# A quantized gated FFN on one core: the gate row fetched by DMA, weight chunks held for x 0, tile 1's results on ScalarE and GpSimd, and the up codes of tile 3 ahead of tile 2's results

## The reference

```
h   = gelu(cond @ W0 + b0);  h = gelu(h @ W1 + b1);  att = softmax(h @ W2 + b2)
y   = einsum(att, weight)[b] @ x[b] + att @ bias_k                      # 128 x 2048, per tile
qg, sg = quant(bf16(y) * inv_gate);   qu, su = quant(bf16(y) * inv_up)  # row max / 127, round, clip
gate = (qg @ w_gate.T) * sg * s_wgate;   up = (qu @ w_up.T) * su * s_wup      # 2048 -> 1024
inter = bf16(clip(silu(gate) * up, -10, 10));   qi, si = quant(inter * inv_inter)
out  = x + (qi @ w_down.T) * si * s_wdown                                     # 1024 -> 2048
```

## Time and profile before

| | |
|---|---|
| median of the timed runs | 824.15 us |
| the profiled execution, as a whole | 823.83 us |
| its span, first to last instruction | 822.0 us |
| TensorE matmul busy | 789.6 us (96%) |
| VectorE busy | 722.2 us (88%) |
| ScalarE busy | 437.4 us (53%) |
| GpSimd busy | 150.7 us (18%) |
| granted TensorE clock, mean | 0.997 of full speed |
| DMA | 117.72 MB, mean 143 GB/s |

### The profile page before, as it was taken

One profiled execution on the slowest core, in us unless ns is written; L12 is line 12 of the kernel. 1 busy time (PEld: TensorE's weight loads), 2 busy tenths in 40 slices (PEclk: granted clock), 3 DMA queues, 4 the chain that ended last, 5 costly groups with the idle time before them and its releaser, 6 DMA issues.

```text
span 822.0 us, 9083 instructions
## 1 busy us (share of the span) xinstructions
PE 789.6 (96%) x3437; PEld 360.1 (44%) x3504; DVE 722.2 (88%) x825; ACT 437.4 (53%) x370; POOL 150.7 (18%) x142
## 2 busy tenths in 40 slices
PE   5689999899999999999999999999999999999997
PEld 2344444344444444444444444444444444444443
DVE  5888898998988888898888899888889888888967
ACT  2556426655556654555665455566555556645441
POOL 3560200222210222221022222012222101222000
PEclk9999999999999999999999999999999999999999
DMA  9995252654544555444435554444545444454332
GB/s 251 232 217 103 52 205 52 166 167 141 160 147 116 109 160 167 141 145 141 138 102 166 161 143 145 122 138 124 167 146 161 141 116 123 147 167 141 100 106 103
DMA packets 158196, 117.72 MB, mean 143 GB/s; under 512 B 147524, under 2 KB 147652, under 8 KB 148807
## 3 DMA queue, kind: packets, MB, share of 16 engines
q1 hardware_dynamic: 156424, 104.55, 42.4%
q0 software_dynamic: 1728, 12.58, 7.7%
HBM read 59.44 MB, written 33.55 MB: 113 GB/s over the span
## 4 chain that ended last, share of the span: by engine, by line
PE 82%; DVE 11%; DMA 3%; ACT 2%; issue 1%; SPq 0%; POOL 0%; DVEq 0%
PE down_ps L584 24%; PE gate_ps L512 23%; PE up_ps L512 23%; PE conv_ps L456 11%; DVE amax L901 3%; DMA wd<-rows 2%; DMA qgT<-qg 1%; ACT qg L690 1%; DVE region L919 1%; DVE region L1012 1%; DVE region L996 1%; DVE region L930 1%; DVE region L1002 1%; DVE region L955 1%; DVE aggw L896 0%
## 5 line engine op out<-in xcount | busy, mean ns | idle before, releaser
L512 PE MATMUL gate_ps<-wg,qgT 128*128 128x512 bf16 x987 | 219.1, 379 | 1.6 <-ACT qgT L714 1.4
L512 PE MATMUL up_ps<-wu,quT 128*128 128x512 bf16 x931 | 215.0, 379 | 3.2 <-ACT quT L722 1.6
L584 PE MATMUL down_ps<-wd,qiT 128*128 128x512 bf16 x884 | 209.1, 379 | 3.6 <-ACT qiT L772 2.1
L901 DVE TENSOR_REDUCE amax<-region 128x1 f32<-128x2048 f32 (+1 forms) x93 | 178.8, 1923 | 1.3
L364 POOL TENSOR_TENSOR prod<-wexp,att_bc 128x1024 f32<-128x1024 f32 x29 | 55.5, 1913 | 558.5 <-DVE region L941 540.5
L512 PEld LDWEIGHTS gate_ps<-wg,qgT 128*128 128x128 bf16 x992 | 96.7, 98 | 119.1 <-issue 3.2
L584 PEld LDWEIGHTS down_ps<-wd,qiT 128*128 128x128 bf16 x912 | 88.9, 98 | 128.2 <-issue 29.7
L512 PEld LDWEIGHTS up_ps<-wu,quT 128*128 128x128 bf16 x960 | 93.7, 98 | 114.8 <-ACT quT L722 1.8
L456 PE MATMUL conv_ps<-xt,aggw 128*128 128x512 f32 x256 | 122.4, 602 | 8.2 <-DMA xt<-x 6.2
L690 ACT ACTIVATE qg<-region,recip 128x2048 f16<-128x2048 f32 x30 | 60.1, 2002 | 129.9 <-DVE recip L911 129.9
L679 ACT ACTIVATE y<-conv_ps,aggb 128x512 bf16<-128x512 f32 x120 | 81.8, 686 | 79.6 <-PE conv_ps L456 75.0
(11 more groups left out here) (117 smaller groups left out, 488.8 us busy)
## 6 DMA issues: line engine op xcount, KB each, us to landing
xt<-x SPq DMA_DIRECT2D x31, 1024.0 KB, 4.8
out<-xt SPq DMA_DIRECT2D x30, 1024.0 KB, 4.0
wg<-w_gateT POOLq DMA_DIRECT2D x4, 1024.0 KB, 13.4
wu<-w_upT POOLq DMA_DIRECT2D x4, 1024.0 KB, 19.0
wd<-w_downT POOLq DMA_DIRECT2D x4, 1024.0 KB, 7.3
out<-xt SPq DMA_DIRECT2D x2, 512.0 KB, 2.7
xt<-x SPq DMA_DIRECT2D x2, 512.0 KB, 3.7
out<-xt SPq DMA_DIRECT2D x4, 256.0 KB, 2.7
```

The source lines that it names most:

```text
L512: last = nc.tensor.matmul(acc[:, n * BANK:(n + 1) * BANK], codes[:, k * P:(k + 1) * P], wts[:, k, n * BANK:(n + 1) * BANK], start=(k == 0) ...
L584: last = nc.tensor.matmul(down_bank(t, c), qiT_at(t)[:, k * P:(k + 1) * P], wd[:, k, c * BANK:(c + 1) * BANK], start=(k == 0), stop=(k == ...
L901: nc.vector.tensor_reduce(amax[:, i:i + 1], src, axis=AX.X, op=ALU.max, apply_absolute_value=True).then_inc(max_ready, 1)
```

## The change

It has four parts.

1. The gate row is no longer in `rows` but an input of its own, and a DMA on SyncE's queue writes it to all 128 partitions, right behind x 0. x 1 comes next, then the remaining rows.
2. GpSimd waits for x 0 before it issues the gate weight chunks, and issues all four at once. The spreads of the other six rows follow.
3. On VectorE tile 1's gate scaling (`quant_g(1)`) comes before the first softmax piece of the later tiles, and on ScalarE the exponential of these comes after tile 1's codes.
4. The results of tile 1 leave VectorE: ScalarE takes each piece out of PSUM times the row scale (`scaled_out`), GpSimd multiplies by the column scale and adds x. These eight GpSimd operations stand ahead of its mixture for tile 5. TensorE turns the up codes of tile 3 right behind down 1, not behind down 2; ScalarE rounds and empties them accordingly, ahead of `conv_out(4)`. Up values of tile 3 get the second half of `region1`, so that only the clip waits for ScalarE to have read `region2`; tile 5's gate scaling then waits for the inner codes of tile 3.

```diff
-        INVG, INVU, SWG, SWU, INVI, SWD = 2, 3, 4, 5, 6, 8
+        INVU, SWG, SWU, INVI, SWD = 1, 2, 3, 4, 6
+        scaled1 = [prod[:, 4 * i:4 * i + 4, :].rearrange("p k o -> p (k o)") for i in range(2)]
 # up_at
+            if t == EARLY:
+                return region1[:, I:H]
 # SyncE, start
             sp.dma_start(xslot(0), x[0, :, :]).then_inc(x_in[0], 16)
-            sp.dma_start(rows_s, rows[:, 0:6 * I]).then_inc(rows_in[0], 16)
-            sp.dma_start(invi_s, rows[:, 6 * I:7 * I]).then_inc(rows_in[1], 16)
+            sp.dma_start(invg_bc[:, :], inv_gate.partition_broadcast(P)).then_inc(invg_in, 16)
+            sp.dma_start(xslot(1), x[1, :, :]).then_inc(x_in[1], 16)
+            sp.dma_start(rows_s, rows[:, 0:4 * I]).then_inc(rows_in[0], 16)
+            sp.dma_start(invi_s, rows[:, 4 * I:5 * I]).then_inc(rows_in[1], 16)
...
-            sp.dma_start(xslot(1), x[1, :, :]).then_inc(x_in[1], 16)
 # SyncE, store(t)
-                sp.wait_ge(result_ready, NC * (t + 1))
+                if t == 1:
+                    sp.wait_ge(second_result, NC)
+                else:
+                    sp.wait_ge(result_ready, NC * t)
 # GpSimd
-            load(wg, w_gateT, 0, wg_in)
-            load(wg, w_gateT, 1, wg_in)
+            pool.wait_ge(x_in[0], 16)
+            for i in range(WCH):
+                load(wg, w_gateT, i, wg_in)
             pool.wait_ge(rows_in[0], 16)
-            spread(invg_bc[:, 0:I], rows_s[:, 0:I])
-            spread(invg_bc[:, I:H], rows_s[:, I:H])
-            load(wg, w_gateT, 2, wg_in)
-            load(wg, w_gateT, 3, wg_in)
...
+            pool.wait_ge(row_spread, SWD)
+            for c in range(NC):
+                cols = slice(c * BANK, (c + 1) * BANK)
+                pool.wait_ge(scaled_ready, NC + c + 1)
+                nc.gpsimd.tensor_tensor(scaled1[c % 2], scaled1[c % 2], swd_bc[:, cols], ALU.mult).then_inc(product_step, 1)
+                pool.wait_ge(product_step, c + 1)
+                nc.gpsimd.tensor_tensor(xcols(1, c), xcols(1, c), scaled1[c % 2], ALU.add).then_inc(second_result, 1)
             for t in range(5, B):
                 if t == 5:
-                    pool.wait_ge(prod_ready, 2)
+                    pool.wait_ge(second_result, NC)
 # TensorE, conv: which PSUM release a piece waits for
                     elif t == 4 and c < 2:
-                        pe.wait_ge(uturn_out, UTURN["i", 1 + c] + 1)
-                    elif t == 5 and c < 2:
                         pe.wait_ge(uturn_out, UTURN["u", 3] + 1 + c)
 # TensorE, order
                 down(1, c)
+            turn_u(3)
             down(2, 0)
             down(2, 1)
             conv(4)
             down(2, 2)
             down(2, 3)
-            turn_u(3)
             up(3)
 # ScalarE
+            def scaled_out(c):
+                if c == 0:
+                    act.wait_ge(iscale_ready, 2)
+                    act.wait_ge(prod_ready, 2)
+                    act.wait_ge(scaled_ready, NC)
+                if c >= 2:
+                    act.wait_ge(second_result, c - 1)
+                act.wait_ge(down_done, NC + c + 1)
+                nc.scalar.activation(scaled1[c % 2], down_bank(1, c), ACT.Copy, scale=tscale(1, 2)).then_inc(scaled_ready, 1)
...
+            quant_g(1)
             act.wait_ge(att_dve, 12)
             nc.scalar.activation(group(eatt, 1), group(logits, 1), ACT.Exp).then_inc(exp_done, 1)
-            quant_g(1)
...
             turned_i(2)
+            scaled_out(0)
+            scaled_out(1)
+            quant_u(3)
+            scaled_out(2)
+            scaled_out(3)
+            turned_u(3)
             conv_out(4)
-            quant_u(3)
-            turned_u(3)
 # VectorE, quant(t), up_out(t), clip(t), down_out(t, c)
+                if t == EARLY + 2:
+                    dve.wait_ge(icodes_ready, EARLY + 1)
...
-                else:
+                elif t > EARLY:
                     dve.wait_ge(ucodes_ready, t + 2)
...
+                if t == EARLY:
+                    dve.wait_ge(ucodes_ready, t + 2)
...
+                if t == 2 and c == 0:
+                    dve.wait_ge(scaled_ready, 2 * NC)
 # VectorE, order
+            quant_g(1)
             softmax_in(1, B - FIRST, 9)
-            quant_g(1)
...
-            for t in range(2):
-                for c in range(NC):
-                    result(t, c)
+            for c in range(NC):
+                result(0, c)
             quant_u(3)
```

More of the change, by code:

```diff
@@ L3, with adaln_ffn @@
 from contextlib import ExitStack
-def adaln_ffn(nc, x, mlp, b2, weightT, w_gateT, w_upT, w_downT, rows, out):
+def adaln_ffn(nc, x, mlp, b2, weightT, w_gateT, w_upT, w_downT, inv_gate, rows, out):
     fp32 = mybir.dt.float32
@@ L184, in adaln_ffn @@
         row_spread = sem("row_spread")
+        invg_in = sem("invg_in")
         ones_set = sem("ones_set")
```

25 lines of the change are left out of this document (12 added, 13 removed).

## The result

The changed kernel took 820.03 us (median of six runs, 818.36 to 821.73), beside 824.08 us for the kernel before on the same chip: a ratio of 0.9947, 95% interval 0.9931 to 0.9962. The forecast was 821.2. The profiled execution took 818.36 us, 5.47 less than the one of before, while the medians are 4.05 apart. The six times are 818.36, 818.38, 820.01, 820.05, 820.16 and 821.73: they lie in steps of about 1.7 us, and the profile shows the lowest.

A forecast was written before the change was run, and what follows sets the result against it. Once the pipeline runs TensorE's matmuls bind, so only its earlier idle and slow time counts: 2.05 us (start) plus 0.9 (middle) is 2.95, giving 820.9 for the profiled execution, median 821.2, range 816.5 to 823.2.

The forecast's parts named there:

- Weight chunks and x 0: Start: with chunks held, x 0 lands at about 8 and conv 0 starts at 10.75, 3.15 us earlier, at full clock.
- Tile 0's codes: VectorE in the start: factor at 19.9, codes, turns and gate 0 6.6 us earlier, a gain that does not last.
- Tile 1's codes: Deciding term: spreads start at about 21.2, product at 29.2, TensorE turns tile 1's codes at 36.2, 3.05 us earlier.
- the walk over boundaries: VectorE's four remaining mixing steps pass one at each boundary between GpSimd's spreads, at 24, 25.6, 27.2 and 28.3.
- The rival with about 6 us for the code: GpSimd's code load by the page: spreads start at 17, tile 1's codes turned at 34.8, 1.4 us more gain.
- The clock: TensorE idle 4.3 us before turning tile 1's codes, then half clock: of the 3.05 us gain 2.05 is kept.
- Rival 1: No slow clock after TensorE's idle time in the start: gain 3.95 us, 820.2 us; chance 0.17.
- Between 45 and 89 us: Order unchanged, so the start's shift is carried; up loads some 3 us later, hidden unless they slip over 5 us.
- The middle: 89 to 150 us: tile 1's results off VectorE, tile 3's up values moved; gain 0.9 us, between -1 and 1.7.
- 2: Spreads start after 23, behind mixing and product: tile 1's codes turned at 31.9, 816 us; chance 0.20 with intermediates.
- 4: GpSimd's eight operations meet VectorE at 3.20 us each, conv 5 10 us late, about 831; 0.08 with milder delays.
- 3: VectorE's mixing delays GpSimd's descriptors, so all chunks and x 2 slip 5 us: 820.8 to 822.3; chance 0.10.

The follow-up runs named there:

- the repeat: The changed kernel run once more, unaltered: median 819.70 us, ratio 0.9940 to the kernel before; its profiled execution took 820.15 us.
- code early: Changed kernel plus one tiny partition_broadcast, read by nothing, on GpSimd ahead of its wait for x 0: 818.67 us.
- mixing held: Changed kernel, but GpSimd's mixing of conv 5's weights also waits for VectorE's product of tile 4: 819.56 us.
- x 2 early: Changed kernel, but the load of x 2 is issued right behind the rows instead of behind gate chunk 0: 820.18 us.
- fillers ahead of turn 0: Unread matmuls in TensorE's idle time before turning tile 0's codes; alone on the changed kernel, with three more before conv 2: 818.99 us; three combined kernels: 817.53 to 818.99.

## Why the prediction was right, and where its terms were off

- **Weight chunks and x 0.** Conv 0 at 10.81 for 10.75, full clock (but see the slow start in the repeat), x 1 no longer waited for: right. That this step carries the change is shown by the kernel without the hold; the prediction had the hold as a term of its own, worth 3.15 us at conv 0, and did not see that four chunks issued at once would cost 10 us without it.
- **Tile 0's codes.** Factor at 19.75 for 19.9: right.
- **Tile 1's codes.** First spread at 20.71 for 21.2, turn 1 at 35.66 for 36.2: gain 3.61 for 3.05. The chain was mis-sized: the spreads took 8.0 us for 9.3, the product started at 27.62 for 29.2, and met a spread itself (3.24 us for 2.3). The size of the spreads isn't the whole of it: in the repeat they took 10.0 us, one of them 3.31, and the product started at 27.03 even so. In the profiles with late spreads the seven mixing steps took anything from 5.31 to 7.72 us, and the walk over boundaries gave only one of the ways. The rival with about 6 us for the code, after the Trainium skill ("GPSIMD Engine Reference", section 2.1), had turn 1 at 34.8; the trace had 9.35 us. And x 2 came at 31.42, not 28.5, so that TensorE's idle time stood mostly ahead of conv 2 and x 2 came next behind VectorE's chain: with x 2 behind chunk 0 the floor of 31.9 for turn 1 was really 34.8, as the kernel with code early shows.
- **The clock.** Charged 1.0 us. The profile has nothing lost, the repeat 1.10 at turn 1 and 1.51 at the next one. Rival 1 (no slow clock, 820.2) and the forecast are not two cases: the same kernel does either from one execution to the next, and the medians, 820.03 and 819.70, lie on the upper of the two steps (819.7 to 820.3).
- **Between 45 and 89 us.** "The shift is carried" failed by 0.96 us: the gain is 3.61 at turn 1 and 4.57 at 52.48. In the kernel before two products of VectorE took 2.79 and 2.74 us beside GpSimd's mixing; after they take 2.29 and 2.28, and TensorE's wait of 0.98 is gone. An equal shift of one engine is not one of two, and a collision is a matter of half a microsecond of phase. The two rows of before:

```profile
42.87 2.79 DVE L919 TENSOR_TENSOR region<-wd,invg_bc 128x2048 f32<-128x2048 bf16 x1 [3.77 <-ACT wd L679]
...
49.51 2.74 DVE L930 TENSOR_TENSOR region<-y,invu_bc 128x2048 f32<-128x2048 bf16 x1
```

- **The middle.** 0.95 before turn 3 (1.16), 1.7 before gate 4 (2.30), 1.2 before down 3 (1.24), six of GpSimd's eight operations undisturbed (the others 1.72 and 1.60): the mechanisms are right. Its sum, 0.9, is 0.2 to 0.5: the collision at tile 4's product, named as a risk, came, and cost 0.2 as the kernel with mixing held shows; that down 0's and up 3's waits reappear at turn 3 and gate 4 was foreseen. From 52.48 on the profile does gain 0.92 us, but 0.80 of it is the shorter wait at conv 6, which the prediction had not counted and the change does not make: that this term came out is luck.
- **The sum.** For the profiled execution the forecast was 820.9, and it took 818.36. The 2.54 us are 0.56 at turn 1, 1.00 of clock charged and not lost, 0.96 between 45 and 89 us, and 0.02 in the middle, conv 6 included. The repeat's profile (820.15) was 0.75 off: it did lose the clock, and there the terms are 0.46, 0.55 and -0.28. The measured median lies 1.7 us above the first profile, which is why the forecast median is off by 1.2 us only.
- **Rivals.** 2 and 4 fell: the first spread was not after 23, and nothing waited for x 5 (conv 5 ran without a gap). 3 fell as put: the chunks were issued from 9.01 to 11.36 beside VectorE's mixing, 2.35 us for four; what made a late chunk was sharing with other transfers. The up loads were issued at 28.70; the prediction had 30.5 and called it some 3 us later than before, where 29.02 against 30.5 is 1.5.

Left open: why the DMA transpose ahead of conv 6 took 0.8 us longer in the profile of before; the slow start of conv 0 in four profiles; and the times one step above the others, 821.73 here and 822.52 in the kernel with mixing held, of which there is no trace (the mean clock of the first, 0.994, is the lowest of its six).

## What to carry to other kernels

A DMA moved ahead is paid by what shares the engines with it: ask which bytes TensorE needs first, and hold the others; here the hold was worth 10 us, and without it the changed kernel was 6 us slower than the kernel before. When the idle time of an engine has no releaser in the profile, take the waits of the code one by one and look which ends just before it: here one that looked like late weights was VectorE, delayed by GpSimd. Where a queue stands idle with nothing to wait for ahead of a kind of GpSimd instruction, issue a tiny one of that kind while the queue waits anyway. And when steps of a scatter are as large as the effect, look in the profiles for what falls on or beside the path (here the clock's slow stretch, and collisions of VectorE and GpSimd) before comparing two of them.

## What the runs showed of the hardware

- Casting loads slow all: 426 GB/s with plain transfers alone and 270 with chunks among them, at a DMA share of 1.0 in both. Counted by bytes read, with two for every byte that a chunk writes, the second is about 410 (an estimate from 0.53 and 0.55 MB in 4 us).
- The time before GpSimd's first spread (7.55 to 10.68 us) is paid once, also ahead of a spread of 128 columns (7.55 to 8.15 us), and four DMA issues behind it don't bring it back.
- A spread of 1024 columns took 1.30 to 1.41, 1.70 or 3.31 to 3.42 us by what VectorE did beside it, and a product of VectorE over 2048 columns 2.28 to 3.79 by what GpSimd did.
- The same DMA transpose took 3.6 to 4.5 us from issue to landing in four profiles.
- The half clock followed an idle time of 2.47 us (behind tile 0's codes) in one execution and of 3.61 us in another of the same kernel, whose gap at the first place was 1.90. The length of the gap doesn't decide it: with x 2 early the same 2.47 us were followed by none.
- With fillers ahead of turn 0 the clock column shows no half clock in three kernels of four, and shows it in the fourth, where turn 0 still waited 1.57 us. In two of the three, conv 0 and conv 1 had taken 9.5 us, so the fillers alone are not shown to be the reason.
- Conv 0 and conv 1 took 7.79 to 7.87 us in seven profiles and 9.46 to 9.58 in four, all at a recorded clock of 1.00.
